# Moving the context statistics of a two-layer attention kernel to the end of the step before, three batches ahead

## What is computed

```
x = x + _L0_xattn_ref(ctx_1024, _layernorm(x), Wq, Wkv, Wo, ln1_w, ln1_b, ln2_w, ln2_b)
x = x + _L0_attn_ref(...)          # state-space scan
x = x + _L0_ffn_ref(...)           # experts
x = x + _L1_xattn_ref(ctx_1024, _layernorm(x), mask, g1, b1, g2, b2, Wq, Wkv, Wout)
x = x + _L1_attn_ref(...)          # state-space block
x = x + _L1_ffn_ref(...)           # fp4 block
```

## Time and profile before

| | us |
|---|---|
| median of 3 runs (lowest, highest) | 2179.64 (2179.64, 2184.43) |
| the profiled execution | 2175.95 |
| its span | 2174.3 |
| first attention loop, first to last `p_lo` | 90.2 to 904.6 |
| second attention loop, first to last `p_lo` | 1220.0 to 1999.5 |

### The profile page before, as it was taken

The page is one execution under the profiler, slowest core; times in us unless marked ns, Lnnn a source line. Parts: engine busy times, 40 slices in busy tenths (PEclk is TensorE's granted clock), DMA queues, the critical chain, the costliest instruction groups (busy, mean ns, idle before and its releaser), DMA issues. The chain is left out here.

```text
span 2174.3 us, 37348 instructions
## 1 busy us (share of the span) xinstructions
PE 2012.8 (93%) x11706; PEld 1090.7 (50%) x11706; DVE 1700.0 (78%) x4108; ACT 1284.3 (59%) x2308; POOL 600.7 (28%) x648
## 2 busy tenths in 40 slices
PE   5899999999999999889798999999999999999886
PEld 4444545353535455433567445454545454544584
DVE  5789797979788887589666877778787979785657
ACT  2376666666666666644323486868687777777211
POOL 3435353534343432059201102121111111110000
PEclk8899999999999999989999899999999999999897
DMA  3222222222222211033104012121111111110100
GB/s 111 81 64 64 65 64 63 64 63 63 63 64 63 91 37 48 9 95 126 48 1 110 5 37 52 31 61 36 35 36 36 36 36 37 36 33 1 27 2 10
DMA packets 148169, 108.91 MB, mean 50 GB/s; under 512 B 120748, under 2 KB 136088, under 8 KB 148024
## 3 DMA queue, kind: packets, MB, share of 16 engines
q1 hardware_dynamic: 148024, 107.26, 17.2%
HBM read 65.15 MB, written 14.29 MB: 37 GB/s over the span
## 5 line engine op out<-in xcount | busy, mean ns | idle before, releaser
L1134 DVE TENSOR_TENSOR x_p_lo<-x_psum,x_p_hi 128x512 f16<-128x512 f32 (+2 forms) x896 | 605.5, 684 | 153.8 <-ACT x_psum L930 141.1
L929 ACT ACTIVATE x_p_hi<-x_psum 128x512 f16<-128x512 f32 (+2 forms) x480 | 287.4, 599 | 303.3 <-PE x_psum L788 301.5
L929 ACT ACTIVATE x_p_hi<-x_psum,x_bcol 128x512 f16<-128x512 f32 (+1 forms) x416 | 288.8, 694 | 139.6 <-PE x_psum L788 137.4
L805 PE MATMUL x_psum<-x_p_hi,x_x_both 128*128 128x512 f16 (+1 forms) x832 | 316.7, 381 | 33.1 <-DVE x_p_lo L1134 32.5
L786 PE MATMUL x_psum<-x_q,x_xT_both 128*128 128x512 f16 x832 | 316.9, 381 | 0.9 <-DMA x_q<-x_shift_rows 0.7
L807 PE MATMUL x_psum<-x_p_hi,x_x_both 128*128 128x512 f16 (+1 forms) x832 | 315.8, 380 | 0.0
L787 PE MATMUL x_psum<-x_q,x_xT_both 128*128 128x512 f16 x832 | 315.8, 380 | 0.0
L806 PE MATMUL x_psum<-x_p_lo,x_x_both 128*128 128x512 f16 (+1 forms) x832 | 315.8, 380 | 0.0
L788 PE MATMUL x_psum<-x_q,x_xT_both 128*128 128x512 f16 x832 | 315.8, 380 | 0.0
L1073 DVE CUSTOM_DVE_ANT_0 x_junk<-x_psum,x_brow 128x512 bf16<-128x512 f32 (+2 forms) x512 | 279.7, 585 | 9.9 <-PE x_psum L852 9.2
L930 ACT ACTIVATE x_psum<-x_psum 128x512 f32<-128x512 f32 (+2 forms) x480 | 286.0, 596 | 0.6
(11 more groups left out here) (450 smaller groups left out, 3256.9 us busy)
## 6 DMA issues: line engine op xcount, KB each, us to landing
x_x_both<-context_rows SPq DMA_DIRECT2D x32, 832.0 KB, 5.4
context_rows<-x_x SPq DMA_DIRECT2D x16, 832.0 KB, 5.7
x_raw<-in_ctx SPq DMA_DIRECT2D x16, 768.0 KB
ssm_c_row<-ssm_bc_rows SPq DMA_DIRECT2D x16, 512.0 KB, 4.1
ssm_b_wide<-ssm_bc_rows SPq DMA_DIRECT2D x7, 512.0 KB, 3.5
x_mrow<-in_mask_BxS_bk SPq DMA_DIRECT2D x16, 200.1 KB
x_Wkv<-in_L_xattn_Wkv SPq DMA_DIRECT2D x4, 512.0 KB, 4.9
x_xT_both<-context_rows SPq DMA_TRANSPOSE x96, 3.7
```

Of the source, the lines that this page charges most:

```text
L805: pe.matmul(out, v_hi, p_hi[r][rows, :], start=start, stop=False)
L929: act.activation(p_hi[r][rows, :], score[r][rows, :], ACT.Exp, scale=SCORE_UNIT, **bias).then_inc(p_hi_ready, 1)
L1134: v.tensor_tensor(p_lo[r][rows, :], score[r][rows, :], p_hi[r][rows, :], ALU.subtract).then_inc(p_lo_ready, 1)
```

## The change

Four things are changed.

1. The `bn_stats` are cut into five parts of 3, 3, 3, 2 and 2 (`STATS_OF`). They and the group with its following operation are made for batch b + **3** in the last five units of step b (23 to 27), each behind the unit's item; the group and line 253's operation stand in unit 27.
2. The nine root operations follow in the next step, in units 0 to 3 (3, 2, 3, 1), ahead of the item. Step 0 still makes all parts of batch 2 in its units 0 to 8, besides the late ones of batch 3. Steps 13 to 15 have no late parts, steps 14 and 15 no statistics.
3. In SP's queue `load_raw` of batch b + 3 stands ahead of `rows`. What it waits for, that batch b + 1 has been normalised, was done in the step before.
4. In both loops the `out` items stand in units 20, 22 and 24.

The diff:

```diff
--- before.py
+++ after.py
@@ -62,7 +62,10 @@
 RSQRT_STEPS = 2 + 4 + 3
 CUBE = 0.375
 NORM_STEPS = KT + 5 + 1 + RSQRT_STEPS
-STATS_PARTS = 4 + 2 + RSQRT_STEPS
+STATS_OF = ((0, 3), (3, 6), (6, 9), (9, 11), (11, KT))
+AGGR = len(STATS_OF)
+ROOTS = AGGR + 2
+STATS_PARTS = ROOTS + RSQRT_STEPS
 
 
 def rsqrt_step(v, k, out, val, t):
@@ -230,11 +233,14 @@
             if part == 0:
                 x_step[0] = Steps(v, norm_steps, n * NORM_STEPS)
                 v.wait_ge(raw_in[par], (i + 1) * 48)
+            if part == ROOTS:
+                x_step[0] = Steps(v, norm_steps, n * NORM_STEPS)
+                x_step[0].n = KT + 5 + 1
             steps = x_step[0]
-            if part < 4:
-                for j in range(4 * part, min(4 * part + 4, KT)):
+            if part < AGGR:
+                for j in range(*STATS_OF[part]):
                     steps.mark(v.bn_stats(xstats[:, j, :], raw[par][:, j, :]))
-            elif part == 4:
+            elif part == AGGR:
                 if not (isinstance(n, int) and n == 0):
                     wait(v, xt_ready, n)
                 wait(v, norm_steps, steps.base + steps.n)
@@ -249,10 +255,10 @@
                 steps.mark(v.scalar_tensor_tensor(xvar[:, :], xm2[:, :], 1.0 / D, xd2[:, :], ALU.mult, ALU.add))
             else:
                 steps.wait()
-                if part == 5:
+                if part == AGGR + 1:
                     steps.mark(v.tensor_scalar(xrv[:, :], xvar[:, :], LN_EPS, None, ALU.add))
                 else:
-                    steps.mark(rsqrt_step(v, part - 6, xr[:, :], xrv[:, :], xrt[:, :]))
+                    steps.mark(rsqrt_step(v, part - ROOTS, xr[:, :], xrv[:, :], xrt[:, :]))
             assert part < STATS_PARTS - 1 or steps.n == NORM_STEPS
 
         def context_normal(pool, wait, n, par):
@@ -330,7 +336,7 @@
 
 
             STATS_WITH = {n: [(b, part) for part in parts] for n, b, parts in (
-                (VF_C, 0, range(0, 4)), (VF_L, 0, range(4, 8)), (K_C, 0, range(8, STATS_PARTS)), (VO + 2, 1, range(0, 4)))}
+                (VF_C, 0, range(0, AGGR)), (VF_L, 0, range(AGGR, ROOTS + 2)), (K_C, 0, range(ROOTS + 2, STATS_PARTS)), (VO + 2, 1, range(0, AGGR)))}
             if masked:
                 STATS_WITH = {}
 
@@ -589,7 +595,7 @@
             if item[0] == "max" and double and len(out[u]) == 1 and item[1] % 4 == 0:
                 double -= 1
             else:
-                u += 1 + {paused: PAUSE[par][0], ("max", 2 * NC_ - 1): PAUSE[par][1]}.get(item, 0)
+                u += 1 + {paused: PAUSE[par][0], ("max", 2 * NC_ - 1): PAUSE[par][1], ("out", 0): 1, ("out", 1): 1}.get(item, 0)
         if not pre:
             out[LAST] = [("lat", 0)]
         return out
@@ -747,11 +753,11 @@
                 if at.has_next2 and masked:
                     wait_alone(sp, bcol_ready, at.b + 1)
                     load_mask(at.b + 2, at.par)
-                if at.has_next:
-                    rows(at)
                 if at.has_next3 and not masked:
                     sp.wait_ge(xt_ready, at.b + 2)
                     load_raw(sp, at.b + 3, at.npar, at.ni + 1)
+                if at.has_next:
+                    rows(at)
                 if at.has_next2:
                     if not masked:
                         store_x(sp, at.b + 2)
@@ -1042,12 +1048,16 @@
 
         @block.vector
         def _(v):
-            def stats_parts(u):
-
-                if u < 4:
-                    return (u,), (4,) if u == 3 else ()
-                parts = [k for k in (2 * u - 3, 2 * u - 2) if k < STATS_PARTS]
-                return parts[:1], parts[1:]
+            def stats_parts(u, at):
+
+                if at.first and at.par == 0:
+                    early = [[k] for k in range(AGGR)] + [[AGGR, AGGR + 1]]
+                    early += [[k, k + 1, k + 2] for k in range(ROOTS, STATS_PARTS, 3)]
+                else:
+                    early = [[ROOTS, ROOTS + 1, ROOTS + 2], [ROOTS + 3, ROOTS + 4], [ROOTS + 5, ROOTS + 6, ROOTS + 7], [ROOTS + 8]]
+                late = {LAST - AGGR + 1 + k: [k] for k in range(AGGR)}
+                late[LAST] += [AGGR, AGGR + 1]
+                return early[u] if u < len(early) else (), late.get(u, ())
 
             def consume(at, item):
                 kind, a = item
@@ -1123,7 +1133,7 @@
                 for item in at.index:
                     consume(at, item)
                     if item == ("q", Q_ITEMS - 1) and not masked:
-                        for part in range(4, STATS_PARTS):
+                        for part in range(AGGR, STATS_PARTS):
                             context_stats(v, wait_alone, 1, 1, 0, part)
 
             def body(at):
@@ -1134,16 +1144,16 @@
                     v.tensor_tensor(p_lo[r][rows, :], score[r][rows, :], p_hi[r][rows, :], ALU.subtract).then_inc(p_lo_ready, 1)
                     if u == 1 and not (at.first and at.par == 0):
                         latents_sums(at.half, 1 - at.par)
-                    soon, later = stats_parts(u) if at.has_next2 and not masked else ((), ())
-                    for part in soon:
+                    two, three = stats_parts(u, at) if not masked else ((), ())
+                    for part in two if at.has_next2 else ():
                         context_stats(v, wait_alone, at.b + 2, at.par, at.i + 1, part)
                     for item in at.items.get(u - LAG, []):
                         if item[0] == "out":
                             project(item[1], aux, at.ready(item), at.i - 1, LATER_PARTS * (at.i + 1))
                         else:
                             consume(at, item)
-                    for part in later:
-                        context_stats(v, wait_alone, at.b + 2, at.par, at.i + 1, part)
+                    for part in three if at.has_next3 else ():
+                        context_stats(v, wait_alone, at.b + 3, at.npar, at.ni + 1, part)
 
             every(v, before, body)
             latents_sums(B * STEPS, 1)
```

## The result

The changed kernel took 2210.88 us (median of 4 runs, 2208.11 to 2216.19), the kernel before 2180.77 (median of 4 runs of the comparison): a ratio of **1.014, 95% interval 1.011 to 1.016**, 30 us slower. The direction was forecast; the size was not. The forecast was 15 us, and 2210.88 lies outside its range of 2170 to 2202. The profiled execution took 2208.11 us (span 2206.4, mean granted clock 0.965, before 0.973).

The account below looks back on a forecast made before the run. The prediction took both loops as a race between PE and DVE, with PE the bound from unit 9 to the end of the `max` items. Parts 1 to 6 gave -10.3 us, part 7 +25.8: +15.5, so 2195 us, range 2170 to 2202.

Parts of the forecast that it names:

- Part 1 to 3: Even steps 2 to 12, PV(0) to PV(18): fewer stalls at the start, at line 1081 and for raw context; -24.1 us.
- Roots dearer than 0.2: Rival, chance 0.05: chained roots keep even starts bound by DVE, part 1 gives 1.2, +7, 2202 us.
- Part 3, raw context: Raw transfers at the head of SP's queue: a transposed-row wait and DVE's raw wait in step 2 go; -2.5 us.
- Part 4, `out` items: Even steps of both loops: PE's 0.3 us waits for the division go; -4.2 us, of which -2.1 in the second loop.
- Part 5 and 7 at even ends: Ends of even steps: late `bn_stats` delay `p_lo`, +6.0 us; the group waits for POOL, 1.9 us a step.
- Part 6 at the four edges: Ends of odd steps at loop edges: 3.4 us of late statistics less 1.2 of cheaper jump, +8.8 us over four.
- part 7: Unit 27: the group waits for POOL operations, 2.4 us in odd and 1.9 in even steps, +25.8 us in all.
- the jump should get cheaper: DVE's branch at the first loop's edges: 4.8 us falls to the second loop's 3.6, with only transposes beside it; -1.2 each.
- No blocking: Rival, chance 0.20: the group slips past POOL, part 7 is zero, the kernel gets faster; -10.3, 2169 us.
- half the blocking: Rival, chance 0.20: only the group's two `TENSOR_TENSOR` wait for POOL, +12 in place of +25.8; 2181 us, no change.
- The edge stays at 4.8: Rival, chance 0.15: the late branch meets straight copy and raw transfers, so the jump keeps its length; +4.8, 2200 us.

Follow-up runs that it names:

- experiment 7: Changed kernel with idle identity matmuls on PE ahead of its wait for `p_lo` of unit 0, to keep the clock up; 2209.11 us, ratio 1.014.
- experiment 2: Kernel before with only two parts of the change, `out` items two units apart and raw context issued first; 2166.70 us, ratio 0.994.
- experiment 9: Changed kernel with GpSimd waiting for `p_lo` of the next step's unit 1, so none of its operations runs beside the group in unit 27; 2228.71 us, ratio 1.022.
- experiment 8: Changed kernel with SyncE waiting in odd steps for the next step's seventh score before issuing the straight copy and raw context; 2210.39 us, ratio 1.015.
- experiment 5: Changed kernel with the group and the operation behind it moved from unit 27 to unit 1 of the next step, `bn_stats` staying late; 2165.01 us, ratio 0.994.

## Why the prediction was right in direction and wrong in size

- **Part 1 to 3, even starts: right, with one term missing.** The stalls of units 1 to 3 and 17 are gone, and line 1091 takes 0.41 us. The gain is 19.2 us in place of 24.1. If the four steps behind an edge took what steps 4 and 6 take in experiment 7 at full clock (29.35 us from PV(0) to PV(18)), it would be 24.6, so the low clock takes back 5.4. "Roots dearer than 0.2" is out too: at full clock PV(0) to PV(9) takes 14.69 us there, and the forecast's 14.3 + 0.6 makes 14.9.
- **Part 3, raw context: right in place, too small by itself.** It gave about 8 us in experiment 2, not 2.5; I had priced two waits, and not the shorter odd ends and starts. How much of the 8 is left in the changed kernel isn't shown: its jumps are not at 4.1 us but at 4.3.
- **Part 4, `out` items: right.** The second loop gained 1.8 us for a forecast of 2.1.
- **Part 5 and 7 at even ends: right.** They cost 14.1 with part 4, forecast 15.3. The blocking is 1.7 us a step (experiment 9), forecast 1.9.
- **Part 6 at the four edges: the first failed step.** The blocking of part 7 was right there: 2.0 a step, forecast 2.4. But "the jump should get cheaper" was wrong: it took 4.24 to 4.35 us, 0.3 less than before on the mean of the four edges and not 1.2. Its reason was that transposes alone leave the jump at 3.6 us; experiment 8 has transposes alone beside it, and it takes 4.3. That is 3.4 us over four edges. And the work ahead of the branch was sized at 3.4 us, the statistics alone. Without any blocking (experiment 9) it is 4.5: the eleven `bn_stats` of units 23 to 26 take 2.4, and from the start of the last `p_lo` to the branch pass 2.2 in place of 0.05, for the `p_lo` itself (0.7), two `bn_stats` (0.5) and the chain of six (1.0). The forecast left out that the last `p_lo` had run during the jump and now stands ahead of it. That is 4.6 more over four edges. At steps 1 and 11, which have no jump, the same work cost 1.1 or 1.2 and not 1.6.
- **The second failed step is a term that the prediction put at nothing without a reason.** It let PE wait 6 us at an edge and took for granted that PE comes back as fast as it left. The granted clock falls to half in six places of the loop, at the four edges and after steps 2 and 6. The starts of the odd steps, for which the forecast had zero, lose 5.0 us, 2.4 of them by the clock (steps 3 and 7), the rest by short waits (PV(0) to PV(4) takes 9.65 us at full clock in place of 9.20). With the 5.4 of the even starts the clock costs about 8 us.
- **The rivals.** "No blocking" and "half the blocking" fell with the rows of lines 249 to 255. "The edge stays at 4.8" was the nearest in mechanism: it stayed at 4.3.
- **The sum.** The forecast's 15.5, and beside it 4.9 at the even starts, 5.0 at the odd starts, 4.6 at the odd ends, -1.2 at the even ends and 3.4 in step 0, the second loop and the stretches outside the loops, make 32.2, and the spans of the two profiles differ by 32.1; the medians differ by 30. Of the 3.4, 2.5 lie in stretches that the change doesn't touch, and over the thirteen profiles the one between the loops alone varies by 6.6. The price of the clock isn't a fixed one either: the places at which it falls differ from kernel to kernel, and one more or less is worth 1.1 to 1.6 us.

*On the rules.* The prediction named the Trainium skill's page "SBUF — State Buffer", section "Who interferes with whom", for a form of which it had no row; the runs now have one: the `SCALAR_TENSOR_TENSOR` form waits too, 0.68 us in place of 0.18 beside line 715 and 1.16 beside line 958. The Trainium skill's page "Runtime: NRT & Kernel Launch", section "Instruction fetch mechanics", says that a taken branch whose target is not at hand has to fetch it before execution can go on; the trace agrees with the wait: 4.3 us of idle DVE behind each taken branch of the first loop, and 0.03 at 747.1, where it ends. That a fetch fills this time is shown by no run here.

What stays open: why the jump takes 4.8, 4.3, 4.1 or 2.9 us in the first loop of different kernels and 3.5 in the second, the transposed copies beside it being the untested candidate; and why the clock falls after even steps 2 and 6 and not after 4, 8 and 10, whose waits are the same. In experiment 8, with these waits unchanged, it falls after 4 and 8 instead.

## What to carry to other kernels

Moving small operations out of a crowded stretch pays only if they land where their engine waits anyway, ahead of the wait and not behind it. With the same two helpful parts in both kernels, worth 14 us by themselves, the statistics at the end of a step made the program 30 us slower and those in idle units 25 us faster. Before a chain of dependent operations goes right ahead of a loop's branch, look at what the sequencer can still run ahead of: the jump's price is added to the chain, not hidden by it, and the operation that used to run during the jump is added too. And when a change lengthens a wait of PE, add the price of a lower clock behind it, and not only the wait.

## What was not expected of the hardware

- The granted clock fell to 0.5 not only behind waits of 6 us but also after steps 2 and 6 behind waits of 0.6, 0.3 and 1.7 us with matmuls between them, and at two edges although 4 of 6 us were filled with idle matmuls.
- The same taken branch cost DVE 2.8 to 4.9 us in the first loop, ACT 0.3. It was cheapest (experiment 5) where it was taken with four instructions not yet started and the DMA engines 2% busy behind it; which of the two counts isn't shown.
- The group of six operations on 13 elements, 1.1 us of busy time, costs 46 us of the program where it stands in unit 27, some 3.5 us for each of its 13 executions.
